# A GNN kernel on one core: GpSimd takes part of the one-hot rows, and the q, k and v products go in f32r parts

## The chip, the cores and the metric

One core of one Trainium2 chip. The metric is the device time of one execution in microseconds; the profiled execution of the kernel before has a span of 487.2 us.

## The reference, cut to what matters

Four graph layers in a row on 512 nodes with 512 features and 16896 edges. What the change touches is the first layer and the table of edges that all layers use:

```
h = relu(layernorm(x))                       # N = 512 nodes, D = 512
q, k, v = h @ Wq + bq, h @ Wk + bk, h @ Wv + bv          # 8 heads of 64
adj = zeros(N, N); adj[src, dst] = 1
scores = q k^T / 8, -1e9 where adj == 0; softmax over heads; times v
... @ Wo, layernorm, feed forward, layernorm
```

Then follow two graph convolutions, one more convolution, and two relational layers that sum 30 basis matrices each into their weights (those matrices are 64 MB, streamed from HBM through the whole kernel).

## The kernel before, in words

**Queues.** Each engine runs one list of instructions written out by hand; they meet in semaphores only. TensorE's list (`pe`) sets the order around the change: `turn` transposes the four blocks of `h`; then comes a loop over 132 chunks of 128 edges (`ECH`). `count(n)` adds one chunk to a table in PSUM bank 7: one bf16 matmul of a 128x128 matrix `hot_d` (a one-hot row of the edge's destination, times a power of two that says which field of the table it belongs to) with a 128x512 matrix `hot_s` (the one-hot row of its source). Both stand in rings of 16 (`HOT`), and a slot is free when the count 16 chunks earlier is done (`hot_used`).

**Who makes the rows.** VectorE (DVE) makes every `hot_s` and, of 132 `hot_d`, the 71 for which `on_act(n)` is false (both in `one_hots`, L722 and L725). ScalarE (ACT) makes the other 61 in two activations each (`distances`, L443, and L468). GpSimd (POOL) makes none; it issues DMAs.

**What stands between the counts.** After the counts 0, 16, 32, ..., 112 TensorE does `qkv_tile(t)`: one 128x512 tile of q (t = 0 to 3) or k (4 to 7) out of four fp32 matmuls (L1280), and then, but for the first, `units(1)`: one MB of basis matrices, read by SyncE's queue into a ring of four (`bring`), in four column-tiled fp32 matmuls (L1197, eight records). ACT takes each finished tile to SBUF (`qk_take`, 14 chunks after it in its own list). After the loop the first half of the table's digits is taken apart by DVE, and the four v tiles are done, two before and two inside the attention steps.

**The start.** DVE computes the norm of `x`, waits for the edge arrays (three DMAs of SyncE's queue, behind the four of `x`), derives the columns from them in eight steps (`edge_step`), then makes `never` (L772) and `bq8` (L774, behind the DMAs of `cols` and `alphas`), and only then the first one-hot rows. ACT copies the transposes to `hT` in fp32 (L395).

**Other products.** All later products of weights already use parts: a float is cut into a high part in f32r and the rest, and hi\*hi + hi\*lo + lo\*hi are three f32r matmuls in place of one in fp32 (`parts_tile`, L1211). ACT makes the high part (L405), DVE the low one (L877).

Of the kernel before, what the change touches and what calls it, by code (L numbers as in the profile page):

```python
# [28 lines left out]
P = 128  # L29
# [20 lines left out]
FIRST_TILE, TILE_EVERY = 0, 16  # L50
TILE_LAG = 14


def act_hots(n):

    return n * 15 // 32
# [44 lines left out]
T_ORDER = ("h1T", "ff1", "ff1_second", "hT2", "agg0", "agg1", "agg2")  # L101
# [12 lines left out]
def build(nc, x, src, dst, etype, weights, rows, cols, alphas, att, basis, scratch, out):  # L114
    with ExitStack() as ctx:
# [71 lines left out]
        x_hi, x_lo = root_hi, root_lo  # L187
        ff1_hi, ff1_lo = (root_hi, root_lo), (y0_hi, y0_lo)
# [83 lines left out]
        with nc.Block() as block:  # L272

            @block.sync
            def _(sp):
# [3 lines left out]
                for i, e in enumerate((src, dst, etype)):  # L279
                    sp.dma_start(edge_i[:, i, :], e).then_inc(sem("edges_loaded"), 16)  # L280
# [35 lines left out]
            def _(pool):  # L316
# [13 lines left out]
                pool.wait_ge(sem("att_loaded"), 16 * 2 * Q)  # L330
                for g in range(1, BATCH):
                    pool.tensor_copy(attw[0:KB, :, g, blk(Q, g)], attw[0:KB, :, 0, 0:Q]).then_inc(
                        sem("att_ready"), 1)
                for i in range(RSLOTS):
                    pool.dma_start(row(ROWS[i]), rows[i, :].partition_broadcast(P)).then_inc(
                        sem(f"row_slot{i}_loaded"), 16)
# [22 lines left out]

                load_weight("f1a")  # L360
                load_weight("f1b")
# [17 lines left out]
            def _(act):  # L379
# [78 lines left out]
                for c in range(C):  # L458
                    turn("hT0", hT, c)
                for n in range(ECH):  # L460
# [10 lines left out]
                    t, at = divmod(n - FIRST_TILE - TILE_LAG, TILE_EVERY)  # L471
                    if at == 0 and 0 <= t < 2 * C:
# [229 lines left out]
            def _(dve):  # L702
# [13 lines left out]
                def one_hots(n):  # L716


                    if n >= HOT:
                        dve.wait_ge(sem("hot_used"), n - HOT + 1)  # L720
                    if not on_act(n):
                        dve.tensor_scalar(hot_d[:, n % HOT, :], iota[:, 0:P], dst_lo[:, n:n + 1],  # L722
                                          weight_f[:, n:n + 1], ALU.is_equal, ALU.mult).then_inc(
                                              sem("hot_ready"), 1)
                    dve.tensor_scalar(hot_s[:, n % HOT, :], iota[:, :], src_f[:, n:n + 1], None,  # L725
                                      ALU.is_equal).then_inc(sem("hot_ready"), 1)
# [19 lines left out]

                for c in range(C):
# [4 lines left out]
                nbias(0, C - 1)  # L752

# [6 lines left out]
                dve.tensor_scalar(rel1, edge_i[:, 2, :], 0.0, None, ALU.not_equal).then_inc(sem("edge_step"), 1)  # L760
                dve.wait_ge(sem("edge_step"), 4)
# [9 lines left out]
                dve.wait_ge(sem("ident"), 2)  # L771
                dve.tensor_scalar(never[:, :], ident[:, :], NEVER, None, ALU.mult).then_inc(sem("never"), 1)  # L772
                dve.wait_ge(sem("cols_loaded"), 32)
                dve.tensor_scalar(bq8[:, :], col("bq", 0, C), HD ** -0.5, None, ALU.mult).then_inc(sem("bq8"), 1)  # L774
# [7 lines left out]
                for n in range(ECH):  # L782
                    one_hots(n)
                    t, at = divmod(n - FIRST_TILE - TILE_LAG, TILE_EVERY)
                    if at == 5 and C <= t < 2 * C:
                        plus_bo(t - C)
# [3 lines left out]
                dve.wait_ge(sem("packed"), 1)  # L790

# [380 lines left out]
            def _(pe):  # L1172
# [93 lines left out]
                def qkv_tile(t):  # L1266

                    which, c = divmod(t, C)
                    w = weight("qkv"[which])
                    if c == 0:  # L1270
                        need_weight(pe, "qkv"[which])
# [5 lines left out]
                    for k in range(C):  # L1277
                        a, b = ((w[:, k, blk(P, c)], hT[:, k, :]) if which < 2 else
                                (hT[:, k, blk(P, c)], w[:, k, :]))
# [3 lines left out]
                first, every = FIRST_TILE, TILE_EVERY  # L1283
# [3 lines left out]
                for n in range(ECH):  # L1287
                    count(n)
                    if n == first:
                        pe.wait_ge(sem("hT0"), C)  # L1290
                    t, at = divmod(n - first, every)
                    if at == 0 and t < 2 * C:
                        qkv_tile(t)
                        if t:
# [338 lines left out]
```

## Time and profile before

| | |
|---|---|
| median of 3 runs | 491.48 us (491.46 to 494.15) |
| profiled execution | 488.97 us, of which 487.2 us span |
| TensorE busy | 442.7 us (91%) |
| VectorE busy | 353.7 us (73%) |
| ScalarE busy | 241.4 us (50%) |
| GpSimd busy | 19.4 us (4%) |
| HBM | 92.45 MB read, 201 GB/s over the span |

The span is what the instructions take from the first to the last; 1.8 us lie around it. The busy shares are means over stages that have different limits, so each stage has to be looked at by itself.

### The profile page before, as it was taken

What the parts mean: (1) busy time and instruction counts of PE and PEld (TensorE: products, weight loads), DVE (VectorE), ACT (ScalarE), POOL (GpSimd) and SP (SyncE); (2) the same over time, 40 slices, a digit from 0 to 9 for tenths busy, and PEclk for the clock granted to TensorE, in tenths of its full rate; (3) what the DMA queues carried; (4) which work ended last, traced back from release to release, by engine and by line L of the source; (5) the groups of instructions that cost most, each with busy time, mean ns of one, the idle gap of its engine ahead of it and who ended that gap; (6) DMA issues with size and microseconds to landing.
All of it is one profiled execution on the core that took longest, in us unless ns stands there. A gap on an engine that the chain in (4) does not pass through costs nothing.

```text
span 487.2 us, 6230 instructions
## 1 busy us (share of the span) xinstructions
PE 442.7 (91%) x2210; PEld 275.4 (57%) x2214; DVE 353.7 (73%) x765; ACT 241.4 (50%) x425; POOL 19.4 (4%) x43
## 2 busy tenths in 40 slices
PE   1699999889877799899999899799989899999997
PEld 1343433344322243577867667578557488888885
DVE  4687887799998869877879684657687767585312
ACT  4697885585786551754225425445562442611210
POOL 3210000001000000100010000000000000000000
PEclk9999999999999999999999999999999899999999
DMA  7992435304999974976149768470797413000002
GB/s 280 339 373 86 173 111 171 109 1 163 367 414 418 394 282 159 398 267 258 77 172 386 275 218 352 174 280 2 291 412 199 172 42 154 3 0 1 0 3 86
DMA packets 18457, 98.16 MB, mean 201 GB/s; under 512 B 3711, under 2 KB 4095, under 8 KB 7935
## 3 DMA queue, kind: packets, MB, share of 16 engines
q1 hardware_dynamic: 14871, 73.58, 40.0%
q0 software_dynamic: 3552, 24.12, 13.3%
q8 instruction: 22, 0.36, 0.3%
q14 instruction: 12, 0.10, 0.1%
HBM read 92.45 MB, written 5.24 MB: 201 GB/s over the span
## 4 chain that ended last, share of the span: by engine, by line
PE 69%; DMA 13%; DVE 11%; ACT 3%; issue 2%; SPq 1%; DVEq 0%; ACTq 0%
PE bank L1211 13%; DMA bring<-in_basis 11%; PE sbank L1528 9%; PE bank L1280 7%; PE sbank L1197 7%; PE bank L1541 6%; PE sbank L1263 6%; PE bank L1423 5%; PE bank L1513 5%; PE bank L1247 3%; DMA alph<-in_alphas 3%; PE bank L1197 3%; PE sbank L1387 2%; PE sbank L1181 2%; PE sbank L1247 2%
## 5 line engine op out<-in xcount | busy, mean ns | idle before, releaser
L725 DVE TENSOR_SCALAR cnt<-iota_row,edge_f 128x512 bf16<-128x512 f16 x132 | 41.5, 352 | 4.5 <-PE sbank L1263 4.5
L1197 PE MATMUL sbank<-bring,attw 120*32 120x512 f32 x320 | 40.4, 616 | 2.2 <-DMA bring<-in_basis 2.2
L1197 PE MATMUL bank<-bring,attw 120*32 120x512 f32 x192 | 24.3, 618 | 8.2 <-DMA bring<-in_basis 8.0
L383 ACT ACTIVATE stat<-stat 128x1 f32<-128x1 f32 x32 | 6.5, 202 | 51.0 <-DVE stat L733 51.0
L1263 PE MATMUL sbank<-cnt,adjT 128*128 128x512 bf16 x128 | 29.4, 381 | 1.9 <-DVE cnt L725 1.3
L1280 PE MATMUL bank<-hT,wring 128*128 128x512 f32 x64 | 30.5, 622 | 0.0
L468 ACT ACTIVATE adjT<-distance,edge_w,edge_f 128x128 bf16<-128x128 bf16 x61 | 29.3, 480 | 1.4 <-PE sbank L1263 1.4
L1130 DVE SCALAR_TENSOR_TENSOR y_lo<-sbank,gate,y_hi 128x512 fp32r<-128x512 f32 x16 | 11.8, 750 | 22.5 <-ACT y_hi L652 22.5
L443 ACT ACTIVATE distance<-iota_row,edge_f 128x128 bf16<-128x128 f16 x61 | 24.4, 401 | 5.1 <-DVE edge_f L769 3.4
L722 DVE TENSOR_SCALAR adjT<-iota_row,edge_f,edge_w 128x128 bf16<-128x128 f16 x71 | 22.2, 313 | 6.3 <-remote 6.3
L1211 PE MATMUL bank<-hT_hi,w_hi 128*128 128x512 f32 x64 | 25.5, 398 | 1.0 <-DVE y_hi L958 0.8
L411 ACT ACTIVATE s<-bank,colsb 128x512 f32<-128x512 f32 x24 | 16.4, 684 | 18.8 <-PE bank L1211 18.8
L1181 PE MATMUL sbank<-ident,hr 128*128 128x128 f32 x64 | 11.9, 321 | 14.9 <-ACT hr L453 7.5
L1211 PE MATMUL bank<-hT_hi,w_lo 128*128 128x512 f32 x64 | 25.0, 391 | 0.0
L1211 PE MATMUL bank<-hT_lo,w_hi 128*128 128x512 f32 x64 | 24.9, 390 | 0.0
L1528 PE MATMUL sbank<-w_hi,xT_hi 128*128 128x512 f32 x64 | 24.9, 389 | 0.0
L1528 PE MATMUL sbank<-w_hi,xT_lo 128*128 128x512 f32 x64 | 24.9, 389 | 0.0
L1528 PE MATMUL sbank<-w_lo,xT_hi 128*128 128x512 f32 x64 | 24.9, 389 | 0.0
L1263 PEld LDWEIGHTS sbank<-cnt,adjT 128*128 128x128 bf16 x132 | 12.3, 98 | 21.7 <-DVE cnt L725 4.4
L1311 PE MATMUL sbank<-qkw 64*128 64x256 f32 x128 | 18.1, 402 | 5.8 <-DVE s L899 5.0
L490 ACT ACTIVATE s<-s 128x1024 f32<-128x1024 f32 x16 | 16.8, 1058 | 11.9 <-DVE s L899 11.4
L652 ACT ACTIVATE y_hi<-sbank,gate 128x512 fp32r<-128x512 f32 x16 | 10.8, 688 | 23.8 <-PE sbank L1528 23.8
(224 smaller groups left out, 1046.3 us busy)
## 6 DMA issues: line engine op xcount, KB each, us to landing
bring<-in_basis SPq DMA_DIRECT2D x63, 1024.0 KB, 8.1
wring<-in_weights POOLq DMA_DIRECT2D x8, 1024.0 KB, 8.8
w_scratch<-stage SPq DMA_DIRECT2D x64, 64.0 KB, 6.9
hT<-in_weights POOLq DMA_DIRECT2D x4, 1024.0 KB, 5.3
landing<-in_weights POOLq DMA_DIRECT2D x4, 1024.0 KB, 8.5
qkw<-w_scratch POOLq DMA_DIRECT2D x2, 2048.0 KB, 8.1
rring<-in_rows POOLq DMA_DIRECT2D x12, 256.0 KB, 8.0
xr<-in_x SPq DMA_DIRECT2D x4, 256.0 KB, 4.0
```

Source lines behind the costliest of these rows:

```text
L443: act.activation(distance[:, i % 2, :], iota[:, 0:P], ACT.Abs, scale=-1.0, bias=dst_lo[:, n:n + 1]).then_inc(sem("distance"), 1)
L468: act.activation(hot_d[:, n % HOT, :], distance[:, i % 2, :], ACT.Relu, scale=minus_w[:, n:n + 1], bias=weight_f[:, n:n + 1]).then_inc(sem ...
L725: dve.tensor_scalar(hot_s[:, n % HOT, :], iota[:, :], src_f[:, n:n + 1], None, ALU.is_equal).then_inc(sem("hot_ready"), 1)
L1197: mm = pe.matmul(unit_bank(b)[32 * j:32 * j + 32, :], attw[0:KB, u // UNITS, g, :], bring[0:KB, u % BATCH, j, :], start=(g == 0), stop=(g ...
L1211: mm = pe.matmul(bank[c][:, :], lhs[:, k, blk(P, c)], rhs[:, k, :], start=(k == 0 and i == j), stop=(k == C - 1 and i == 1))
L1247: mm = pe.matmul(bank[first_bank + c][:, :], x[:, k, blk(P, c)].bitcast(dt), counts[:, k, :], start=(k == 0 and i == 0), stop=(k == C - 1 ...
L1263: pe.matmul(bank[7][:, :], hot_d[:, n % HOT, :], hot_s[:, n % HOT, :], start=(n == 0), stop=(n == ECH - 1)).then_inc(sem("hot_used"), 1)
L1280: mm = pe.matmul(bank[at][:, :], a, b, start=(k == 0), stop=(k == C - 1))
L1423: mm = pe.matmul(bank[c][:, :], (ff1_hi, ff1_lo)[i][k // C][:, k % C, blk(P, c)], weight_parts("f2a" if k < C else "f2b")[j][:, k % C, :], ...
L1513: mm = pe.matmul(bank[c][:, :], (xT_hi, xT_lo)[i][:, k, blk(P, c)], (root_hi, root_lo)[j][:, k, :], start=(k == 0 and i == j), stop=False)
L1528: mm = pe.matmul(bank[C + c][:, :], (xT_hi, xT_lo)[i][:, k, blk(P, c)], (w_hi, w_lo)[j][:, rel * C + k, :], start=(k == 0 and i == j), sto ...
L1541: mm = pe.matmul(bank[c][:, :], counts[:, k, blk(P, c)], y[:, k, :].bitcast(dt), start=False, stop=(rel == RELS - 1 and k == C - 1 and i = ...
```

## The change

1. Of the 132 `hot_d`, ACT makes `n * 5 // 16` = 41 and GpSimd the other 91; DVE makes none. TensorE waits for `pool_hot_ready` too.
2. `qkv_tile` is twelve f32r matmuls in place of four fp32 ones. The low parts of `h` are made by DVE (`h0T_lo`), the high ones by ACT, which now turns block c right after the norm of block c + 1. The weight of q is cut by GpSimd (high) and DVE (low) ahead of the loop, those of k and v by ACT and DVE inside the loop.
3. The tiles of q and k come after the counts 0, 8, 16, 28, 46, 64, 84 and 104; ACT takes each 7 chunks later in its list.
4. The three edge DMAs are issued by ACT's queue, ahead of its first square root. The five row DMAs of GpSimd and the copies of `attw` stand inside its loop. `never` and `bq8` move to chunk 8 of DVE's loop.
5. The loads of `f1a` and `f1b` change places; DVE waits for all k tiles before it writes the digits.

```diff
-FIRST_TILE, TILE_EVERY = 0, 16
-TILE_LAG = 14
+TILE_AT = (0, 8, 16, 28, 46, 64, 84, 104)
+TILE_LAG = 7
 def act_hots(n):
-    return n * 15 // 32
+    return n * 5 // 16
...
+        h0_hi, h0_lo = y1_lo, hT_r
+        qkv_parts = {"q": (y0_hi, w0_hi), "k": (y0_lo, w0_lo), "v": (w0_hi, w1_hi)}
...
@@ SyncE's list @@
-                for i, e in enumerate((src, dst, etype)):
-                    sp.dma_start(edge_i[:, i, :], e).then_inc(sem("edges_loaded"), 16)
...
@@ GpSimd's list @@
+                need_weight(pool, "q")
+                for k in range(C):
+                    pool.tensor_copy(qkv_parts["q"][0][:, k, :], weight("q")[:, k, :]).then_inc(sem("q_hi"), 1)
+                pool.wait_ge(sem("edge_step"), 8)
+                for n in range(ECH):
+                    if n == HOT:
+                        pool.wait_ge(sem("att_loaded"), 16 * 2 * Q)
+                        for g in range(1, BATCH):
                            pool.tensor_copy(attw[0:KB, :, g, blk(Q, g)], ...)
+                    i, at = divmod(n - 2 * HOT, 4)
+                    if at == 0 and 0 <= i < RSLOTS:
+                        pool.dma_start(row(ROWS[i]), ...)
+                    if on_act(n):
+                        continue
+                    if n >= HOT:
+                        pool.wait_ge(sem("hot_used"), n - HOT + 1)
+                    pool.tensor_scalar(hot_d[:, n % HOT, :], iota[:, 0:P], dst_lo[:, n:n + 1],
+                                       weight_f[:, n:n + 1], ALU.is_equal, ALU.mult).then_inc(
+                                           sem("pool_hot_ready"), 1)
...
@@ ACT's list @@
+                def high_part(name, k):
+                    if k == 0:
+                        need_weight(act, name)
+                    if name == "v":
+                        act.wait_ge(sem("q_psum"), C)
+                    act.copy(qkv_parts[name][0][:, k, :], weight(name)[:, k, :]).then_inc(sem("kv_hi"), 1)
+                for i, e in enumerate((src, dst, etype)):
+                    act.dma_start(edge_i[:, i, :], e).then_inc(sem("edges_loaded"), 16)
+                    if c:
+                        turn("hT0", h0_hi, c - 1)
+                turn("hT0", h0_hi, C - 1)
+                    if n - 2 * HOT in (0, 2, 4, 6):
+                        high_part("k", (n - 2 * HOT) // 2)
+                    if n - 4 * HOT - 12 in (0, 4, 8, 12):
+                        high_part("v", (n - 4 * HOT - 12) // 4)
...
@@ DVE's list @@
-                    if not on_act(n):
-                        dve.tensor_scalar(hot_d[:, n % HOT, :], ...)
+                def low_part(name, k):
+                    hi, lo = qkv_parts[name]
+                    dve.wait_ge(*((sem("q_hi"), k + 1) if name == "q" else
+                                  (sem("kv_hi"), "kv".index(name) * C + k + 1)))
+                    dve.tensor_tensor(lo[:, k, :], weight(name)[:, k, :], hi[:, k, :].bitcast(F32),
+                                      ALU.subtract).then_inc(sem("qkv_parts"), 1)
+                def h0T_lo(c):
+                    dve.wait_ge(sem("T_hi"), c + 1)
+                    dve.tensor_tensor(h0_lo[:, :, blk(P, c)], bank[4 + c % 2] ..., h0_hi ..., ALU.subtract)
@@ h0T_lo(0) stands after nbias, h0T_lo(1) after edge step 4; before the loop: @@
+                low_part("q", 0); low_part("q", 1); h0T_lo(2); h0T_lo(3); low_part("q", 2); low_part("q", 3)
+                    if n == HOT // 2:  # never, bq8
+                    if n - 2 * HOT - 8 in (0, 2, 4, 6):
+                        low_part("k", (n - 2 * HOT - 8) // 2)
+                    if n - 5 * HOT in (0, 4, 8, 12):
+                        low_part("v", (n - 5 * HOT) // 4)
+                    if n - 112 in (0, 4, 8, 12):
+                        plus_bo((n - 112) // 4)
+                dve.wait_ge(sem("k_psum"), C)   # ahead of the digits
...
@@ TensorE's list @@
-                    pe.wait_ge(sem("hot_ready"), 2 * (n + 1) - act_hots(n + 1))
+                    pe.wait_ge(sem("hot_ready"), n + 1)
+                    pe.wait_ge(sem("pool_hot_ready"), n + 1 - act_hots(n + 1))
                     for k in range(C):
-                        mm = pe.matmul(bank[at][:, :], a, b, start=(k == 0), stop=(k == C - 1))
+                        pe.wait_ge(sem("qkv_parts"), which * C + k + 1)
+                        for i, j in ((0, 0), (0, 1), (1, 0)):
+                            ...
+                            mm = pe.matmul(bank[at][:, :], lhs, rhs, start=(k == 0 and i == j),
+                                           stop=(k == C - 1 and i == 1))
```

## Rows read from the trace of the kernel before

**Rows 1.** Busy time by stretch: us, then each engine's busy time (instructions), clock, DMA

```profile
17.90:84.30 66.40, 65.25 (x252) 26.48 (x260) 53.70 (x208) 52.80 (x130) 4.04 (x8) 1.00 0.56 198
...
121.00:175.00 54.00, 44.56 (x327) 16.58 (x324) 47.56 (x53) 38.48 (x47) 0.00 (x0) 0.97 0.99 400
```

**Rows 2.** Chain of waits, 17.6 to 28 us: start, us, what

```profile
4.49 13.20 DMA alph<-in_alphas
...
17.71 0.17 DVE bq L774
...
18.41 0.61 PE sbank L1263
19.02 5.15 PE bank L1280 x8
```

**Rows 3.** Chain of waits over the whole span, some of its longest pieces

```profile
27.62 3.43 PE bank L1280 x8
31.06 1.00 PE sbank L1197 x8
32.21 3.40 PE sbank L1263 x15
...
278.16 11.15 PE bank L1211 x48
```

**Rows 4.** Groups by line, 18.4 to 84.2 us: busy us, mean ns, idle before and its releaser

```profile
L725 DVE TENSOR_SCALAR cnt<-iota_row,edge_f 128x512 bf16<-128x512 f16 x131 | 41.1, 352 | 4.5 <-PE sbank L1263 4.5
...
L468 ACT ACTIVATE adjT<-distance,edge_w,edge_f 128x128 bf16<-128x128 bf16 x61 | 29.3, 480 | 1.4 <-PE sbank L1263 1.4
L443 ACT ACTIVATE distance<-iota_row,edge_f 128x128 bf16<-128x128 f16 x59 | 23.6, 400 | 1.7
L722 DVE TENSOR_SCALAR adjT<-iota_row,edge_f,edge_w 128x128 bf16<-128x128 f16 x70 | 21.9, 313 | 6.3 <-remote 6.3
```

**Rows 5.** Timeline of VectorE, 20 to 24 us, while its loop runs freely

```profile
20.51 0.32 DVE L722 TENSOR_SCALAR adjT<-iota_row,edge_f,edge_w 128x128 bf16<-128x128 f16 x1
20.73 0.62 DVE L725 TENSOR_SCALAR cnt<-iota_row,edge_f 128x512 bf16<-128x512 f16 x2
21.25 0.32 DVE L722 TENSOR_SCALAR adjT<-iota_row,edge_f,edge_w 128x128 bf16<-128x128 f16 x1
```

**Rows 6.** Timeline of GpSimd, 0 to 30 us

```profile
1.59 0.51 POOL L320 MEMSET zeros<- 128x512 bf16 x1
...
2.44 0.29 POOL L324 TENSOR_SCALAR_AFFINE_SELECT ident<-ident 128x128 f32<-128x128 f32 x1 [0.16 <-POOL ident L322]
...
21.80 1.11 POOL L332 COPY attw<-attw 120x16 f32<-120x16 f32 x3 [16.59 <-DMA attw<-in_att]
22.86 2.98 POOL L335 DMA_DIRECT2D rring<-in_rows x5
```

**Rows 7.** Timeline, 278 to 285 us: a weight is cut into its parts

```profile
278.62 2.21 ACT L405 CAST w_hi<-hT 128x512 fp32r<-128x512 f32 x4
...
279.73 2.49 DVE L877 TENSOR_TENSOR w_lo<-hT,w_hi 128x512 fp32r<-128x512 f32 x4
```

**Rows 8.** Timeline of the start, 0 to 22 us

```profile
9.35 0.21 DVE L738 TENSOR_SCALAR stat<-stat 128x1 f32<-128x1 f32 x1 [0.16 <-ACT stat L383]
12.50 0.23 DVE L755 CAST edge_f<-edge_i 128x132 f32<-128x132 int32 x1 [2.94 <-DMA edge_i<-in_etype]
...
13.91 0.23 DVE L769 TENSOR_SCALAR edge_f<-edge_w 128x132 f32<-128x132 f32 x1
```

**Rows 9.** DMA issues at 2.9 to 3.4 us: KB, us to landing

```profile
wring<-in_weights POOLq DMA_DIRECT2D x1, 1024.0 KB, 7.8
```

**Rows 10.** Chain of waits, 84 to 125 us

```profile
87.12 3.63 PE bank L1280 x8
...
93.02 1.23 DVE softmax_tmp L824
...
124.88 10.20 DMA bring<-in_basis
```

More of the change, by code:

```diff
@@ L329, in _ @@
                     pool.dma_start(weight(WEIGHTS[i]), weights[i]).then_inc(sem(f"weight_{i}_loaded"), 16)
[L330 to L336, printed above, removed]
+                need_weight(pool, "q")
[6 more added lines that the diff above has]
+                        for g in range(1, BATCH):
+                            pool.tensor_copy(attw[0:KB, :, g, blk(Q, g)], attw[0:KB, :, 0, 0:Q]).then_inc(
+                                sem("att_ready"), 1)
+                    i, at = divmod(n - 2 * HOT, 4)
+                    if at == 0 and 0 <= i < RSLOTS:
+                        pool.dma_start(row(ROWS[i]), rows[i, :].partition_broadcast(P)).then_inc(
+                            sem(f"row_slot{i}_loaded"), 16)
+                    if on_act(n):
[5 more added lines that the diff above has]
+                                           sem("pool_hot_ready"), 1)
                 def load_weight(name):
@@ L358, in load_w @@
                     pool.dma_start(qkw[:, :, :], scratch[layer]).then_inc(sem("w_loaded"), 16)
+                load_weight("f1b")
                 load_weight("f1a")
-                load_weight("f1b")
                 load_row("g2", "v")
@@ L457, in _ @@
                 distances(0)
-                for c in range(C):
-                    turn("hT0", hT, c)
                 for n in range(ECH):
@@ L752, in _ @@
                 nbias(0, C - 1)
+                h0T_lo(0)
                 dve.wait_ge(sem("edges_loaded"), 48)
@@ L770, in _ @@
                 dve.wait_ge(sem("iota"), 1)
[L771 to L774, printed above, removed]
+                low_part("q", 0)
+                low_part("q", 1)
+                h0T_lo(2)
+                h0T_lo(3)
+                low_part("q", 2)
+                low_part("q", 3)
                 def plus_bo(c):
@@ L783, in _ @@
                     one_hots(n)
-                    t, at = divmod(n - FIRST_TILE - TILE_LAG, TILE_EVERY)
-                    if at == 5 and C <= t < 2 * C:
-                        plus_bo(t - C)
+                    if n == HOT // 2:
+                        dve.wait_ge(sem("ident"), 2)
+                        dve.tensor_scalar(never[:, :], ident[:, :], NEVER, None, ALU.mult).then_inc(sem("never"), 1)
+                        dve.wait_ge(sem("cols_loaded"), 32)
+                        dve.tensor_scalar(bq8[:, :], col("bq", 0, C), HD ** -0.5, None, ALU.mult).then_inc(
+                            sem("bq8"), 1)
+                    if n - 2 * HOT - 8 in (0, 2, 4, 6):
[4 more added lines that the diff above has]
+                        plus_bo((n - 112) // 4)
                 dve.wait_ge(sem("hot_used"), ECH)
@@ L1268, in qkv_tile @@
                     which, c = divmod(t, C)
-                    w = weight("qkv"[which])
-                    if c == 0:
-                        need_weight(pe, "qkv"[which])
+                    w = qkv_parts["qkv"[which]]
                     if which == 1:
@@ L1277, in qkv_tile @@
                     for k in range(C):
-                        a, b = ((w[:, k, blk(P, c)], hT[:, k, :]) if which < 2 else
-                                (hT[:, k, blk(P, c)], w[:, k, :]))
-                        mm = pe.matmul(bank[at][:, :], a, b, start=(k == 0), stop=(k == C - 1))
+                        pe.wait_ge(sem("qkv_parts"), which * C + k + 1)
+                        for i, j in ((0, 0), (0, 1), (1, 0)):
+                            h = (h0_hi, h0_lo)[i]
+                            lhs, rhs = ((w[j][:, k, blk(P, c)], h[:, k, :]) if which < 2 else
+                                        (h[:, k, blk(P, c)], w[j][:, k, :]))
+                            mm = pe.matmul(bank[at][:, :], lhs, rhs, start=(k == 0 and i == j),
+                                           stop=(k == C - 1 and i == 1))
                     mm.then_inc(sem("qkv"[which] + "_psum"), 1)
-                first, every = FIRST_TILE, TILE_EVERY
                 pe.wait_ge(sem("ident"), 2)
@@ L1288, in _ @@
                     count(n)
-                    if n == first:
+                    if n == 0:
                         pe.wait_ge(sem("hT0"), C)
[L1291 to L1294, printed above, removed]
+                    if n in TILE_AT:
+                        qkv_tile(TILE_AT.index(n))
+                        if n:
                             units(1)
```

13 lines of the change are left out of this document (7 added, 6 removed).

## The prediction

> **What bounds the kernel now.** I read four views in this order. First the busy time by stretch [rows 1]: from 17.9 to 84.3 us TensorE is busy 65.25 of 66.4 us, VectorE 53.7, ScalarE 52.8, GpSimd 4.0. This is the stretch of the loop over chunks, and TensorE sets its length. Then the chain of waits [rows 2, 3]: from 18.41 us on it runs on TensorE alone, in a pattern of a q or k tile (3.43 us), a unit of basis matrices (1.00) and some 16 counts (15 take 3.40, about 0.22 each). The sum closes: 132 counts at 0.22 = 29; seven tiles at 3.43 and a first one of 5.15 = 29.2; eight units = 8; together 66 us. Then the groups by line [rows 4]: VectorE's one-hot rows wait for free ring slots (4.5 and 6.3 us idle), so the makers of rows are ahead. Last, the start [rows 2, 8]: the loop could not begin before 18.41 us, because `bq8` (17.71) waited for a tiny DMA that landed 13.20 us after its issue. Behind the loop follow the attention steps, and from 124.88 us on a stretch in which the DMAs of the basis are the limit [rows 1, 10]: 0.99 of the DMA engines, begun by TensorE's fourth group of units. It begins when the attention step before it is done and lasts as long as its bytes do, so an earlier end of the loop moves all that follows by the same amount.
>
> **Tiles in f32r parts (on the path).** 48 f32r matmuls took 11.15 us [rows 3], 0.232 each, so 12 take 2.79 us where four fp32 ones took 3.43: 0.64 less a tile. The first tile ran slow before (5.15 us [rows 2], 1.72 more than its kin), right after TensorE's idle time of the start; that idle time stays, so I keep the surcharge. Eight tiles: 8 x 0.64 = **-5.1 us**.
>
> **The v tiles.** Four more. The first (3.63 us at 87.12 [rows 10]) is on the chain, which reaches the first maximum at 93.02: **-0.8 us**. The other three stand beside VectorE's chain of softmax steps: nothing.
>
> **Making the parts (beside, while the cover holds).** ACT copies eight blocks for k and v at 0.55 [rows 7], 2.21 for four, 4.4 us, and loses 20 of its 61 rows, which are worth 0.40 + 0.48 = 0.88 busy each [rows 4], about -17 us. VectorE makes low parts at 0.62 each [rows 7]: eight inside the loop, 5.0 us, and loses 71 rows at 0.22 [rows 5], 15.8 us. If there is no contention both become freer, and cost nothing.
>
> **The start.** VectorE is done with the norm at 9.56 [rows 8]. From there it has: four low parts of the transposes (4 x 0.62 = 2.5), the eight steps on edges (12.50 to 14.14, 1.6), four low parts of q (2.5), one row of sources (0.27). Without a gap the first count starts at 16.4. Do the inputs come in time? The weight of q landed at 2.96 + 7.8 = 10.8 [rows 9]; GpSimd's copy of 128x512 costs at least the 0.51 of a memset of that size [rows 6] and I allow twice that, so its fourth block stands at 13 to 15 us, and is used last, at about 15.5. The edge arrays, landed by 12.5 before, are now issued about 1.9 us earlier, and wanted at 10.2. The last transposes wait in turn for VectorE's first two low parts, which costs a gap of some tenths. GpSimd starts its rows here too and may delay the low parts (below). So the first count comes between 16.4 and 18.4; I take 17.4, **-1.0 us**. `never` and `bq8` are moved behind row 8, where the late DMA is covered by 8 counts and a tile.
>
> **The rows of GpSimd (the open price).** 91 `tensor_scalar` of 128x128. The trace has none on this engine. Nearest from below: the same shape in one pass, affine_select, 0.29 us, with VectorE idle; from above: three COPYs of 16 columns beside a running VectorE took 1.11 us, 0.37 each [rows 6], and 112 further columns at the rate of the memset (0.51 for 512) add 0.11: 0.48. Two column operands and a change of type could double the 0.48, so the ends are 0.29 and 1.0. I take 0.45. What can the loop bear? The tight part is from count 28 on: before it tiles stand close (0, 8, 16, 28), and the ring of 16 fills. From there TensorE has 104 counts (22.5), five tiles (13.9) and five units (5.0), 41.3 us, in which the makers must bring chunks 44 to 131, 88 of them. GpSimd has 60 or 61 of these, so it may take 41.3 / 60 = 0.69, less the row DMAs that fall in (five at 0.6 [rows 6], in part before): **0.67 us each**. 0.45 fits. At the start it makes 11 rows, then waits for the DMAs of `attw`, there by 21.8 [rows 6]; count 16 comes after two more tiles, at about 29 us, so that wait is covered. ACT: 41 rows spaced by 0.81 to 0.88, 36 us, plus 4.4 of parts, 5.5 of `qk_take`, 0.6 of staging: 47 of 60 us.
>
> **Waits on TensorE.** Each count gets one more wait. 61 of the counts had a second one already and the 16 counts of a group still took about 0.22 each [rows 3], so I take nothing; the upper bound is 132 pieces of 0.05 like the handoffs in the chain, 6.6 us, were none of them hidden. The exchange of `f1a` and `f1b` and the wait for the k tiles ahead of the digits cost nothing: `f1a` is first cut three attention steps after both loads were issued, and the last k tile now ends 27 counts before the digits.
>
> **Sum.** -5.1 - 0.8 - 1.0 = -6.9 us. The profiled execution took 488.97 (487.2 span and 1.8 around); 482.1 after it. The median of the runs lies 2.5 above the profiled one, so 491.48 - 6.9 = **484.6 us**.
>
> **Rival 1: VectorE and GpSimd take turns.** Three copies of 16 columns took 0.37 each beside VectorE, where 128 columns took 0.29 in its absence, so each waited 0.1 to 0.25 us, about one instruction of VectorE [rows 5, 6]; VectorE's own spacing (0.74 for three instructions) did not grow visibly, but those copies were tiny. If a GpSimd row holds VectorE back for its whole length x, the tight part needs 88 x 0.26 + 5.0 + 2.5 of other VectorE work (a little less of it falls in: 6.0) + 60x = 28.9 + 60x against 41.3: free up to x = 0.21, +5.0 us at 0.29, +9.8 at 0.37. That gives 489.6 to 494.4. Against it: part of both instructions' length is not traffic (a one-column memset already takes 0.1 in this trace), so the exclusive shares are perhaps 0.2 and 0.15 to 0.2, and the sum stays just inside 41.3. The Trainium skill, page "SBUF — State Buffer", section "Who interferes with whom", speaks for this rival: it says that VectorE in its two-port modes, and a VectorE instruction with two SBUF inputs against a GpSimd one that reads SBUF, lock GpSimd out for the whole instruction and the other way round. By that rule taken literally the result is 489.6 or above; the copies above agree with the one direction, and no row shows the other.
>
> The Trainium skill, page "GPSIMD Engine Reference", section "Engine selection", calls one-input work on GpSimd roughly line-rate; by it the price would lie at the low end, and GpSimd itself would not be the bound.
>
> **Rival 2: GpSimd is simply slow (the other side).** If a row costs p alone, the tight part lasts 60p + 1.2 for the row DMAs. Break-even with the gain of 6.9 is at p = 0.78, slower by over 1% begins at 0.87; at 1.0 the loop ends 19.9 us later than forecast, 504.5. For it: a copy of only 16 columns took 0.41 in the mean on this engine. Against it: the affine_select of full shape in 0.29.
>
> **Rival 3: the start or the waits eat it.** The low parts of q come late behind GpSimd's copies and rows (first count at 19 to 20), or the third wait slows the counts by some hundredths: +2 to +6, 486.6 to 490.6.
>
> **How the numbers follow.** Chances: forecast 0.50 (482.8 to 486.5), rival 1 0.26 (486.5 to 494), rival 2 0.16 (491 to 505), rival 3 0.08. About 1% (4.9 us) is what a measurement of this kernel can tell from none. Faster by over 1% is below 486.6: the forecast's 0.50 and 0.03 of rival 1. Within 1%: 0.29. Slower, above 496.4: 0.18, most of rival 2 and the worst of rival 1. The range of 8 in 10 leaves out the fast tail and the slower half of rival 2: 482.5 to 497.
>
> **What would show it.** A tile's twelve matmuls in 2.8 us; the loop from about 17.4 to 78 us with TensorE busy over 95% of it. GpSimd's spacing of rows: below 0.67 and idle on `hot_used` for the forecast; near 0.69 or more with TensorE waiting on GpSimd's rows for rival 2. For rival 1, VectorE's spacing of rows of sources above 0.40 in the stretch without TensorE's pauses, and TensorE idle before counts. The first maximum at about 86.1 us, which was 93.02; all stages from 121 us on unchanged in length but shifted. If those later stages change their length, or the weight of q lands later than 10.8, the prediction is wrong in a way that I have not priced.

## The result and the profile after

The changed kernel took 507.71 us in the median of four runs (506.25 to 509.92), the kernel before 492.58 us (491.46 to 494.15) beside it: ratio 1.031, 95% interval 1.0254 to 1.0363. It is slower by 3.1%, where 484.6 us had been forecast and 497 was the upper end. The profiled execution took 508.46 us, its span is 506.7, 19.5 more than before.

Busy time by stretch of the kernel after (length, PE, PEld, DVE, ACT, POOL, then clock, DMA share, GB/s), which answers to [rows 1]:

```profile
18.00:40.00 22.00, 21.72 (x92) 13.48 (x93) 14.85 (x47) 9.74 (x23) 21.90 (x29) 1.00 0.73 287
40.00:60.00 20.00, 16.18 (x69) 7.32 (x68) 13.87 (x36) 10.73 (x26) 19.84 (x24) 0.91 0.48 158
60.00:80.00 20.00, 15.70 (x72) 7.21 (x71) 14.93 (x42) 11.94 (x30) 20.00 (x24) 1.00 0.34 110
80.00:100.00 20.00, 15.70 (x53) 6.80 (x53) 8.75 (x25) 6.45 (x16) 20.00 (x23) 0.83 0.18 62
```

GpSimd is busy in 81.7 of these 82 us. TensorE is busy nearly all the time up to 40 us and in some four fifths of it from there on; its granted clock falls to 0.91 and 0.83 in two of the stretches in which it is kept waiting, where it was 1.00 in [rows 1]. VectorE and ScalarE do less than before. So the loop has a new bound, and the chain of waits of the kernel after (start, us, what) says from when:

```profile
18.28 0.61 PE sbank L1316
18.89 5.12 PE bank L1334 x12
24.01 1.81 PE sbank L1316 x8
25.82 2.73 PE bank L1334 x12
...
35.12 2.70 PE sbank L1316 x12
37.81 2.77 PE bank L1334 x12
40.58 1.00 PE sbank L1249 x8
41.58 1.42 PE sbank L1316 x6
43.00 3.35 POOL adjT L348 x3
46.35 0.56 POOL rring L342
...
46.97 1.71 POOL adjT L348 x2
48.68 0.55 POOL rring L342
...
49.28 51.08 POOL adjT L348 x58
...
100.49 0.59 PE sbank L1316 x2
...
104.01 2.95 PE bank L1334 x12
...
109.24 1.23 DVE softmax_tmp L876
```

Up to 43.00 us the pattern is that of [rows 3], on TensorE alone. At count 35 the stock of rows is used up, and from there the chain runs on GpSimd: 63 rows and two row DMAs up to 100.35 us. The groups by line of the page give the price of a row (busy us, mean ns, idle before and its releaser):

```profile
L348 POOL TENSOR_SCALAR adjT<-iota_row,edge_f,edge_w 128x128 bf16<-128x128 f16 x91 | 82.3, 912 | 1.2 <-DVE edge_f L808 0.9
L749 DVE TENSOR_SCALAR cnt<-iota_row,edge_f 128x512 bf16<-128x512 f16 x132 | 45.4, 407 | 20.8 <-PE sbank L1316 20.7
L1316 PE MATMUL sbank<-cnt,adjT 128*128 128x512 bf16 x132 | 36.8, 392 | 16.9 <-DVE cnt L749 10.2
```

912 ns, and GpSimd never waits for a free slot: its idle time before rows is the 1.2 us at the start. VectorE waits 20.7 us for slots instead, so its rows are ahead. The third group names VectorE as the releaser of TensorE's waits, though VectorE was well ahead (48 of its rows stood at 43 us, where count 35 was due); a count waits for several makers, and the chain shows the one that was late. The 91 rows began at 14.36 us: with 82.3 us of rows, five row DMAs at 0.55 and the copies of `attw` the engine is done at 100.4.

The last count starts at 100.7 us (before 83.8), the first maximum at 109.24 (93.02 [rows 10]). Of the 19.5 us of span, 16.2 are there already; the rest comes further on, told with the last three runs below.

### The profile page after: what moved, and what is told of

Read it like the earlier page. It is cut to its first block, busy times and chain, and to the rows that moved or that the text cites. A ratio compares the mean times of both kernels' runs of the same rounds, so it can differ in the third digit from the quotient of the medians.

```text
span 506.7 us, 6399 instructions
## 1 busy us (share of the span) xinstructions
PE 450.5 (89%) x2262; PEld 289.9 (57%) x2262; DVE 358.1 (71%) x710; ACT 229.3 (45%) x393; POOL 103.6 (20%) x138
## 4 chain that ended last, share of the span: by engine, by line
PE 58%; DVE 17%; POOL 11%; DMA 7%; ACT 4%; issue 2%; DVEq 0%; SPq 0%; ACTq 0%
PE bank L1263 11%; POOL adjT L348 11%; PE sbank L1581 9%; DMA bring<-in_basis 6%; PE bank L1594 6%; PE sbank L1249 5%; PE bank L1476 4%; PE bank L1566 4%; PE bank L1299 3%; PE bank L1334 3%; PE bank L1249 2%; PE sbank L1440 2%; DVE stat L754 2%; PE sbank L1316 2%; PE sbank L1233 2%
## 5 line engine op out<-in xcount | busy, mean ns | idle before, releaser
L348 POOL TENSOR_SCALAR adjT<-iota_row,edge_f,edge_w 128x128 bf16<-128x128 f16 x91 | 82.3, 912 | 1.2 <-DVE edge_f L808 0.9
L749 DVE TENSOR_SCALAR cnt<-iota_row,edge_f 128x512 bf16<-128x512 f16 x132 | 45.4, 407 | 20.8 <-PE sbank L1316 20.7
L1316 PE MATMUL sbank<-cnt,adjT 128*128 128x512 bf16 x132 | 36.8, 392 | 16.9 <-DVE cnt L749 10.2
L1364 PE MATMUL sbank<-qkw 64*128 64x256 f32 x128 | 22.0, 470 | 6.4 <-DVE s L951 5.6
L1364 PEld LDWEIGHTS sbank<-qkw 64*128 64x128 f32 x128 | 13.3, 223 | 18.5 <-issue 11.0
L518 ACT ACTIVATE s<-s 128x1024 f32<-128x1024 f32 x16 | 16.9, 1058 | 13.1 <-DVE s L951 12.5
L680 ACT ACTIVATE y_hi<-sbank,gate 128x512 fp32r<-128x512 f32 x16 | 10.8, 688 | 23.8 <-PE sbank L1581 23.8
L1249 PEld LDWEIGHTS sbank<-bring,attw 120*32 120x32 f32 x320 | 8.2, 111 | 21.9 <-issue 18.3
L356 POOL DMA_DIRECT2D hT<-in_weights x4 | 2.1, 533 | 87.3 <-DVE w_lo L929 87.3
```

Source lines behind the costliest of these rows:

```text
L348: pool.tensor_scalar(hot_d[:, n % HOT, :], iota[:, 0:P], dst_lo[:, n:n + 1], weight_f[:, n:n + 1], ALU.is_equal, ALU.mult).then_inc(sem("p ...
L518: act.activation(sc, sc, ACT.Exp).then_inc(sem("exped"), 1)
L1249: mm = pe.matmul(unit_bank(b)[32 * j:32 * j + 32, :], attw[0:KB, u // UNITS, g, :], bring[0:KB, u % BATCH, j, :], start=(g == 0), stop=(g ...
L1316: pe.matmul(bank[7][:, :], hot_d[:, n % HOT, :], hot_s[:, n % HOT, :], start=(n == 0), stop=(n == ECH - 1)).then_inc(sem("hot_used"), 1)
L1364: pe.matmul(sbank[:, place_of(h), :], kT[at:at + HD, h // 2, blk(P, m)], qT[at:at + HD, h // 2, blk(NH, half_n)], start=(a == 0), stop=Fal ...
```

## The experiments

Small kernels first, for the price of a row; then parts of the change; then other shares of the work.

**m1, the price by itself.** This kernel leaves out the network and only copies `x`; besides, GpSimd makes rows of several kinds, alone and beside VectorE. A column operand is one value for each partition, read from a tile; an immediate is a constant in the instruction.

```diff
+ # A 24x tensor_scalar 128x128 f16->bf16, two columns   B one column   C immediate
+ # D 24x tensor_copy   E 8x as A, 128x512   F as A, fp32
+ # G as A beside VectorE's rows of 512   H as A beside VectorE's fp32 tensor_tensor
```

> Not the network: a small kernel that only copies x to the output and times GpSimd's row by itself, 24 rows of 128 columns in each stretch. A: as in the changed kernel (f16 in, bf16 out, two column operands), VectorE idle. B: one column operand. C: one immediate. D: a copy. E: 512 columns. F: fp32 in and out. G: as A, beside VectorE making 128x512 rows of sources. H: as A, beside fp32 subtractions of VectorE. Theory 1 (the row is dear in itself): A is spaced by 0.8 to 0.9 us, G by no more than 0.15 more, and B, C or D show which part of the instruction costs it. Theory 2 (GpSimd and VectorE take turns): A is spaced by 0.3 to 0.6 us and only G and H come to 0.9; VectorE's rows in G are spaced by far more than the 0.26 us they have alone.

The timeline of that kernel (start, us, engine, operation, count), GpSimd's blocks in order and VectorE's beside them:

```profile
2.21 18.58 POOL L70 TENSOR_SCALAR pa<-iota_row,dst,w 128x128 bf16<-128x128 f16 x24
20.88 13.87 POOL L76 TENSOR_SCALAR pb<-iota_row,dst 128x128 bf16<-128x128 f16 x24
34.84 13.78 POOL L81 TENSOR_SCALAR pc<-iota_row 128x128 bf16<-128x128 f16 x24
48.69 5.76 POOL L86 CAST pd<-iota_row 128x128 bf16<-128x128 f16 x24
54.56 16.45 POOL L91 TENSOR_SCALAR pe<-iota_row,dst,w 128x512 bf16<-128x512 f16 x8
71.11 18.58 POOL L97 TENSOR_SCALAR y<-iota,dst,w 128x128 f32<-128x128 f32 x24
...
89.73 4.29 DVE L117 TENSOR_SCALAR va<-iota_row,dst 128x512 bf16<-128x512 f16 x16 [89.73 <-POOL y L97]
94.05 19.39 DVE L121 TENSOR_SCALAR vb<-iota_row,dst 128x512 bf16<-128x512 f16 x64
94.12 21.53 POOL L103 TENSOR_SCALAR pg<-iota_row,dst,w 128x128 bf16<-128x128 f16 x24 [4.43 <-DVE va L117]
...
118.21 12.68 DVE L130 TENSOR_TENSOR vc<-xr,iota 128x512 f32<-128x512 f32 x20
```

Alone a row costs 18.58 / 24 = 0.774 us with two column operands, 0.58 with one or with an immediate, and a copy of the same shape 0.24. Four times the columns cost 2.06 us: (2.056 - 0.774) / 384 = 3.34 ns a column. From f16 to bf16 or in fp32 it costs the same. Beside VectorE's rows it is 21.53 / 24 = 0.90, as in the kernel, and VectorE's go from 4.29 / 16 = 0.268 to 19.39 / 64 = 0.303: three of them to a GpSimd row, each held back by 0.035, so a GpSimd row delays VectorE by 0.1. Of the 0.912 us in the kernel 0.774 are the instruction's own, and 0.13 to 0.14 come from company. Beside fp32 subtractions seven rows took 13.20 us, 1.9 each, and VectorE kept its 0.634.

**e1, only the rows.** The kernel before with GpSimd's 91 rows and ACT's 41, its fp32 tiles left as they were.

```diff
-    return n * 15 // 32
+    return n * 5 // 16
 # GpSimd's loop as in the change; DVE's hot_d removed
+                    pe.wait_ge(sem("hot_ready"), n + 1)
+                    pe.wait_ge(sem("pool_hot_ready"), n + 1 - act_hots(n + 1))
```

> The kernel before, fp32 tiles and its own order of tiles, with only the makers changed: GpSimd 91 rows of destinations, ScalarE 41, VectorE none. If GpSimd's pace alone sets the loop (91 rows at 0.88 to 0.91, from about 14 us on, plus 3 us of DMA issues), the loop ends at 98 to 102 us instead of 84 and the time is 505 to 510 us, the same as the whole change. If the turns with the added fp32 subtractions were a good part of the cost, it would be well below, 498 or less.

505.88 us against 490.67, ratio 1.030 (1.0225 to 1.0374). The rows alone bring as long a time as the whole change. But the last count is at 95.3 us, 5.4 earlier than with the whole change and earlier than I had expected; the first maximum is at 104.56, and some 4 of the 15 us come behind it. The group of rows:

```profile
L345 POOL TENSOR_SCALAR adjT<-iota_row,edge_f,edge_w 128x128 bf16<-128x128 f16 x90 | 76.7, 860 | 0.3
```

GpSimd doesn't wait for slots here either (0.3 us of idle time), and a row costs 860 ns in place of 912; 52 ns in each of 91 rows are 4.7 of the 5.4 us. What e1 leaves out is the work on the parts, fp32 subtractions of VectorE among it. In m1 three of those went by in one GpSimd row of 1.9 us; twelve on the parts of weights would so make four rows dearer by 1 us each, an estimate of 4 us. No run takes this work away alone.

**e2, only the parts; e3, three makers.** The kernel after, but with the rows shared otherwise.

```diff
+def pool_hots(n):
+    return (n - act_hots(n)) * 4 // 7        # e2: 0
-    return n * 5 // 16
+    return n * 11 // 32                      # e3; e2 keeps 5 // 16
+ # DVE makes what is neither ACT's nor GpSimd's
```

> The changed kernel, but VectorE makes the 91 rows of destinations of GpSimd (ScalarE keeps 41); all the rest of the change stands. If the f32r parts and the new start are worth what I took for them (6.9 us) and only GpSimd's rows undid it: 485 to 488 us, with the loop's end at 78 to 80 us; VectorE's own work in the tight part (88 x 0.26 + 60 x 0.22 + 6 = 42 us against TensorE's 41) costs about 1. If the parts bring nothing (waits on TensorE, the start), 491 or more.

> The changed kernel with the rows of destinations dealt three ways: ScalarE 45, GpSimd 49, VectorE 38. GpSimd's 49 rows at 0.9 us are 44 us in a loop of 60, so it no longer sets the pace; VectorE has 132 x 0.3 + 38 x 0.24 + 8 = 57 us of 60. Theory 1 (own price, little lock): TensorE is the bound again, 484 to 487 us. Theory 2 (turns, each GpSimd row holds VectorE back for much of its length): VectorE falls behind, 490 us or more.

e2: 493.62 us, ratio 1.0054 (1.0015 to 1.0092). I had expected a gain, and it is a small loss. Its groups by line from 15 to 100 us:

```profile
L765 DVE TENSOR_SCALAR cnt<-iota_row,edge_f 128x512 bf16<-128x512 f16 x132 | 43.4, 353 | 0.4 <-remote 0.4
L762 DVE TENSOR_SCALAR adjT<-iota_row,edge_f,edge_w 128x128 bf16<-128x128 f16 x91 | 28.7, 315 | 2.3 <-PE sbank L1333 2.3
```

VectorE makes 223 rows here and is idle before them for 2.7 us in all; before it was 10.8 [rows 4]. Its rows stand on the chain of waits from 17.7 to 28.5 us. So VectorE is what TensorE waits for, as GpSimd was, and the tiles' gain has nowhere to go: last count at 84.4 us. e3 with 45 rows by ACT, 49 by GpSimd and 38 by VectorE: 489.22 us, ratio 0.998 (0.995 to 1.0009), last count at 82.2 us, between my two theories. A GpSimd row took 1152 ns there:

```profile
L360 POOL TENSOR_SCALAR adjT<-iota_row,edge_f,edge_w 128x128 bf16<-128x128 f16 x49 | 56.0, 1152 | 8.4 <-PE sbank L1333 5.8 <-remote 1.6 <-DVE edge_f L824 0.8
```

**e7, a cheaper row.** The kernel after with one comparison in GpSimd's row; it leaves out the multiplication by the weight, so the table holds no usable counts, and the kernel's own test of the table is changed to let it go on.

```diff
-                                       weight_f[:, n:n + 1], ALU.is_equal, ALU.mult).then_inc(
+                                       None, ALU.is_equal).then_inc(
...
-                dve.tensor_scalar(flag[:, :], bank[0][0:1, 0:1], float(EDGES), None, ALU.is_equal).then_inc(
+                dve.tensor_scalar(flag[:, :], bank[0][0:1, 0:1], 0.0, None, ALU.is_ge).then_inc(
```

> The changed kernel as it is (GpSimd 91 rows), but its row is one comparison with one column operand: the multiplication by the edge's weight is left out, and the test of the table is made to pass, so the counts are meaningless and only the time counts. In the small kernel this row took 0.58 us alone in place of 0.77. If GpSimd's own price is all of the loss, the loop ends at 91 x 0.65 + 3 + 14.4 = 77 to 84 us and the time falls by some 15 us to that of the kernel before or below. If something else in the change costs (third wait on TensorE, f32r tiles, the start), more than 498 us remain.

494.87 us (three runs), ratio 1.007 (1.0034 to 1.0106). The group of rows from 15 to 100 us:

```profile
L348 POOL TENSOR_SCALAR adjT<-iota_row,edge_f 128x128 bf16<-128x128 f16 x91 | 65.3, 731 | 2.3 <-PE sbank L1316 2.1
```

912 - 731 = 181 ns less for each of 91 rows is 16.5 us, and the last count starts 15.3 us earlier (100.7 to 85.4). By this the price moves the end of the loop as 85 rows would (15.3 / 0.181), near to all 91 and not the 60 of the part that I had called tight. GpSimd now waits 2.1 us for free slots, which it never did before.

**m2, what VectorE does to other kinds.** Again a small kernel that only copies `x`; all of GpSimd's blocks run beside VectorE's rows.

```diff
+ # beside VectorE: 16x one column, 16x immediate, 24x copy, 5x 128x512, 12x two columns
```

> The second small kernel, each stretch of GpSimd beside a free run of VectorE's 128x512 rows (spaced 0.30 us there). In the first one a row with two column operands lasted exactly three VectorE instructions (0.906 beside rows of 0.302, 1.90 beside subtractions of 0.634). Theory (each operand that GpSimd fetches waits for one VectorE instruction to end): one column operand 0.60 us, an immediate 0.30 to 0.60, a copy 0.30, 512 columns 2.1 to 2.4, and beside VectorE rows of 128 columns (0.22 us) a row with two operands 0.77 to 0.88. Rival (a constant surcharge of 0.13 us for company): 0.71, 0.70, 0.37, 2.2 and 0.90.

The rows with one column took 10.64 / 16 = 0.66 us, with an immediate 0.63, with 512 columns 11.53 / 5 = 2.3 and with two columns, beside VectorE's rows of 128 columns, 0.89: 0.05 to 0.25 more than alone and not rounded up to whole instructions of VectorE, so the theory that GpSimd falls in step with VectorE fell, and the rival of a constant 0.13 did too. The copies did something else. Timelines of GpSimd and VectorE, from 32 us:

```profile
32.15 6.38 POOL L81 CAST pd<-iota_row 128x128 bf16<-128x128 f16 x1 [2.31 <-DVE va L110]
```

```profile
32.00 6.38 DVE L113 TENSOR_SCALAR ve<-iota_row,dst 128x512 bf16<-128x512 f16 x24
```

One copy that costs 0.24 alone lasted through all 24 rows that VectorE had queued; the other 23 ran after them.

**e4 and e6, ACT takes more.** As e3, with other shares (ACT, GpSimd, VectorE): 49, 20, 63 and 49, 0, 83.

```diff
-    return n * 11 // 32
+    return n * 12 // 32
-    return (n - act_hots(n)) * 4 // 7
+    return (n - act_hots(n)) * 1 // 4        # e6: 0
```

> The changed kernel with ScalarE making 49 rows of destinations, GpSimd 20 and VectorE 63. In the small kernel a GpSimd row advanced in step with VectorE (three VectorE instructions long) and delayed it by 0.10 us. Theory (every maker below the pace of TensorE): VectorE has 132 x 0.26 + 63 x 0.22 + 8 + 20 x 0.1 = 58 us, ScalarE 49 x 0.81 + 10.5 = 50, GpSimd 20 x 1.1 = 22, TensorE 60: the loop ends at 78 to 80 us and the time is 4 to 6 us below the kernel before. Rival (the ring of 16 is too short for VectorE at 97% of TensorE's pace, so its pauses are not made up): 82 us and 1 to 3 us below.

> As the variant with few rows on GpSimd, but GpSimd makes none: ScalarE 49, VectorE 83. VectorE has 132 x 0.26 + 83 x 0.22 + 8 = 60.6 us against TensorE's 60 and no slack. If VectorE's total sets the time, it ends the loop at 81 to 83 us, and is 1 to 3 us slower than with 20 rows on GpSimd; if GpSimd's rows cost VectorE as much as they save it (0.22 each), the two are equal.

e6: 491.40 us, ratio 1.0013 (0.9976 to 1.005), last count at 83.4 us, so with no rows on GpSimd the change gives nothing that can be told. e4: last count at 82.8 us, and yet 495.40 us, ratio 1.0082 (1.0053 to 1.0111). I had expected a gain of 4 to 6 us, and e6 to be the slower of the two. The profiled execution of e4 was the fastest of its five runs (491.59 us), so no trace of mine shows where the others lost their time.

**e5 and e10, the high parts moved.** Shares 53, 19, 60; the high parts of q are made by ACT in the start, those of k and v by GpSimd in its loop. In VectorE's list the third low part of q stands before the last one of `h`. e10 is e5 word for word, on another chip.

```diff
-                    pool.tensor_copy(qkv_parts["q"][0][:, k, :], weight("q")[:, k, :])
+                    act.copy(qkv_parts["q"][0][:, k, :], weight("q")[:, k, :])
+                    if n - 2 * HOT in (-8, -6, -4, -2):      # GpSimd
+                        high_part("k", (n - 2 * HOT + 8) // 2)
```

> The changed kernel with ScalarE 53 rows, GpSimd 19, VectorE 60; GpSimd makes the high parts of k and v (0.6 us a block) in place of ScalarE, ScalarE those of q in place of GpSimd, so that nothing of GpSimd runs beside VectorE's steps on the edges. Theory (GpSimd's copies stretched those steps from 0.22 to 0.6 us and cost the start what I expected of it): the first count comes at 17.0 to 17.6 us in place of 18.3, and the time is 1 us below the variant with few rows on GpSimd. Rival: the transposes' low parts bound the start and nothing moves.

> The variant with the high parts moved once more, word for word, in five rounds: its first ratio was 0.996 (0.9914 to 1.0006), while its loop ended 3.8 us earlier and its first maximum came 4.5 us earlier than in the profile of the kernel before. If that gain holds to the end, the ratio is 0.991 to 0.995; if the later stages give it back, 0.998 or more.

Ratios 0.996 (0.9914 to 1.0006) and 0.9969 (0.9936 to 1.0002). That lies between my two theories for e10. The start is the clear part. Timeline of VectorE's steps on the edge arrays, the kernel after with GpSimd's casts of the weight of q beside them:

```profile
11.04 2.40 POOL L332 CAST y_hi<-wring 128x512 fp32r<-128x512 f32 x4 [5.80 <-DMA wring<-in_weights]
11.06 0.22 DVE L794 TENSOR_SCALAR dst_part<-edge_i 128x132 int32<-128x132 int32 x1
11.20 0.63 DVE L796 TENSOR_SCALAR dst_part<-edge_i 128x132 int32<-128x132 int32 x1
11.76 0.64 DVE L798 TENSOR_SCALAR edge_f<-edge_i 128x132 f32<-128x132 int32 x1
```

and e10 without them:

```profile
10.63 0.22 DVE L818 TENSOR_SCALAR dst_part<-edge_i 128x132 int32<-128x132 int32 x1
10.77 0.22 DVE L820 TENSOR_SCALAR dst_part<-edge_i 128x132 int32<-128x132 int32 x1
10.91 0.22 DVE L822 TENSOR_SCALAR edge_f<-edge_i 128x132 f32<-128x132 int32 x1
```

Here it is VectorE that is held up: a step beside the casts lasts about as long as a cast (2.40 / 4 = 0.60 us). With the casts gone the first count starts at 16.8 us in e10 and 17.2 in e5, where it was 18.0 to 18.3 in three profiles with GpSimd's casts and 91 rows (e7, b3 and the kernel after); the last one at 80.5 and 80.0, the first maximum at 89.1 and 88.5.

**e8, more for GpSimd; e9, the tiles spread.** Both from e5: GpSimd also adds the row of `bo` to `h` in four fp32 sums; or ACT 57, GpSimd 18, VectorE 57 and tiles spaced more widely.

```diff
+ # e8
+                        pool.tensor_tensor(hr[:, c, :], hr[:, c, :], row("bo"), ALU.add)
+ # e9
-TILE_AT = (0, 8, 16, 28, 46, 64, 84, 104)
+TILE_AT = (0, 8, 16, 28, 47, 67, 88, 110)
```

> The variant with the high parts moved, and GpSimd also adds the row of bo to h at chunks 68, 76, 84 and 92 in place of VectorE at 112 to 124. Theory (VectorE at 97% of TensorE's pace, its last sums stand where TensorE has only counts left): the last count 1 to 2 us earlier, at 78 to 79 us, 485 to 488 us in the median, 3 us or more below the kernel before. Rival (GpSimd's fp32 sums hold VectorE back as long as they save it): no change from the variant without, 489.

> The variant with the high parts moved, with four more rows on ScalarE (57; GpSimd 18, VectorE 57) and the last four tiles spread evenly to the loop's end (after counts 47, 67, 88 and 110 in place of 46, 64, 84 and 104), so that TensorE leaves fewer bare counts at the end, which VectorE can't follow. Theory (VectorE's rate is enough in the mean, and only the tail starves TensorE): the last count at 78.5 to 79.5 us in place of 80.0, 487 to 489 us, 2.5 to 4 us below the kernel before. Rival (the mean rate is the limit): the last count stays at 80 us or later.

e8: ratio 0.9988 (0.9959 to 1.0016), last count at 82.7 us, where I had expected 78 to 79 and e10 has 80.5: the sums took work from VectorE, but its rows of sources became slower, 383 ns in the mean after 366 in e5. e9: ratio 0.9974 (0.9938 to 1.0011), last count at 80.0 us, as in e5. The spacing and the four more rows of ScalarE together don't move the end. That is what the rival said (the makers' mean rate is the limit), but with two things changed at once e9 doesn't prove it.

**b1, b2, b3, the same kernels again.** All versions above that end their loop earlier gained less than that. Between the fourth group of units and the next in the chain of waits the kernel before has 69.2 us, the one after 71.1 and e10 70.4. Is that the spread from one execution to the next?

```diff
 # b1, b2: the kernel before; b3: the kernel after; nothing changed
```

> The kernel before, word for word, for a second profile. In its first profile the stretch from the first units after the loop to the 28th unit took 59.1 us from the 12th on, and in ten profiles of variants 59.9 to 62.3, although nothing in that stretch differs but its start. Theory (the stretch varies from execution to execution, and the first profile of before, 488.97 us against a median of 491, had a short one): 60 to 62 us here. Rival (an earlier or later end of the loop changes how the stretch goes, and a part of each gain is given back there): 59.1 again, within 0.5.

> The kernel before, word for word, a third profile. As for the second: 60 to 62 us from the 12th to the 28th unit if the stretch varies by itself, 59.1 within 0.5 if it does not.

> The changed kernel, word for word, a second profile. The rows of GpSimd: 91 at 0.90 to 0.92 us, the last count at 100 to 101.5 us again (the loop does not vary, all of the spread of the time stands behind it); 506 to 510 us.

The two ends of the stretch in the chain of waits, b1 and then b3:

```profile
122.57 3.62 PE bank L1197 x32
191.00 3.62 PE bank L1197 x32
```

```profile
136.78 3.62 PE bank L1249 x32
206.77 3.62 PE bank L1249 x32
```

68.4 us (b2 68.5) and 70.0. Three profiles of the kernel before lie at 68.4 to 69.2, and the twelve of the kernel after and its variants at 69.9 to 72.3. Two profiles of one kernel differ by up to 1.1 there (71.1 and 70.0 for the kernel after), but the two groups don't overlap, so it is not spread alone: some 1 to 3 us are given back there. Which change does it is not shown. All twelve kernels have another loop, and all of them, e1 too, issue the five row DMAs and the copies of `attw` inside GpSimd's loop; no run has only the one or the other. The stretch after it is spread: from the units at 289 us to the `x32` row at 357 the kernel before took 67.7, 69.2 and 69.0 us, the one after 69.4 and 69.3. b3 reproduces the loss, 506.47 us against 490.98 and 489.97, with 909 ns a row and the last count at 100.0 us.

## Why the prediction was wrong, step by step

**What bounds the kernel.** Right: the chain was on TensorE in the loop, and with other shares it ends earlier (e10: last count at 80.5 against 83.8), though by less than the 5 to 6 us forecast.

**Tiles in parts.** Right. On the chain each took 2.73 to 2.77 us, forecast 2.79. The first took 5.12 against 5.15 [rows 2] in this profile, which looks as if nothing had been gained there, but it varies from one execution to the next. The same tile in b3:

```profile
18.70 4.23 PE bank L1334 x12
```

The chains of ten profiles with twelve f32r matmuls have 3.9 to 5.1 us there, 4.5 in the mean; four with fp32 (the kernel before, b1, b2, e1) have 4.8 to 5.7, 5.3 in the mean. So by the means the first tile gained its 0.64 too, and that nothing of it shows in one profile was chance. What varies is how many of the twelve matmuls start 0.43 us apart, and not 0.23. Two tiles of the loop show the same 0.43 at their start, at 48.9 to 51.3 and 85.1 to 88.8 us, after counts for which TensorE had waited; there the granted clock is 0.50, the lower of its two levels (1.2 and 2.4 GHz). In the first tile the clock row reads 1.00, so for that tile the cause is not shown. The v tile is right within 0.1: 2.95 after 3.63 [rows 10].

**Making the parts.** Right that ACT has room (it went to 53 and 57 rows in e10 and e9). The cover for VectorE was GpSimd: with all 91 rows on VectorE it is gone, and e2 has no gain.

**The start.** Forecast 17.4, measured 18.28, against 18.41 before. The norm was done at 10.41 instead of 9.56, the first block of `x` having landed at 4.45 us instead of 3.96 and VectorE having waited for the second (the edge DMAs are issued beside them now; no run moves these alone). Then GpSimd's casts stretched three of VectorE's steps as shown, by 1.2 us in sum. I had allowed for a delay by rows, not by casts; with 16.8 and 17.2 in e10 and e5 the 17.4 was sound without them.

**Waits on TensorE.** Right: eight counts took 1.81 us, 0.226 each as in [rows 3], each with the added wait.

**The rows of GpSimd: the step that failed.** I took 0.45 us and measured 0.91. The value was taken from copies and an affine_select as the nearest rows, and neither was near: m1 shows that on this engine the operands set the price (copy 0.24, one column 0.58, two 0.77). The upper end, 1.0, held, and rival 2 named the mechanism. How much a dear row costs was mis-sized too. Rival 2's formula, 60p + 1.2, gives 55.2 us at p = 0.9 against 41.3, 13.9 more than forecast: 489 + 7 = 496 for the profiled execution, and 508.5 came. It assumed a full ring at count 28, that is, 30 rows of GpSimd by 36 us; from 14.4 us on GpSimd had made 22 by then. So the engine never gets ahead of its ring, and all 91 rows count: with 14.4 us of start and 3.7 of other work, 18.1 + 91p = 100 at 0.9, against a forecast end of 78. The point up to which it is free, (78 - 18.1) / 91 = 0.66, agrees with my 0.67; the slope above it is 91, not 60. e7 measured 85.

**Rival 1.** The contention is real, but it acts the other way round. What it takes from VectorE, 0.1 us for a row, is small. What it takes from GpSimd, 0.13 to 0.14 us for a row, falls on the engine at the bound: with m1's 0.774 the same sum gives 18.1 + 91 x 0.774 = 88.5 us for the end of the loop, with 0.912 it gives 101. By this estimate 12.6 us of the delay are company; alone, a row's own price would have ended the loop some 5 us later than before (83.8). So a price measured alone would have told the direction, and under a third of the 16.9 us. The Trainium skill, page "SBUF — State Buffer", section "Who interferes with whom", tells of a lock for the whole instruction. For GpSimd's casts beside VectorE's steps (0.22 to 0.64 us) the traces agree; the copy (6.38 us) was shut out too, but through 24 instructions and not one. For rows with column operands no such lock shows: VectorE's went from 0.268 to 0.303 beside GpSimd ones of 0.9. Whether these rows run in one of the two-port modes that the section speaks of, no run here shows. The other page I had named, "GPSIMD Engine Reference", section "Engine selection", calls one-input work roughly line-rate; the copy agrees (0.24 us, VectorE's row of that shape 0.22 [rows 5]), the one-input row with two column operands doesn't, 0.774.

**Later stages only shifted.** Nearly: of 19.5 us, 16.2 are there at the first maximum, 1.9 come in the DMA-bound stretch (69.2 to 71.1) and 1.7 between 289 and 357 us, which b1 and b2 show as spread. The prediction had named a change of length there as a sign of something not priced. What makes the former longer in every variant stays open. In the traces single units and single attention steps jump by 2 to 3 us, as if the loads and the steps of some 10 us paced each other anew; no run here isolates that.

**A better version.** e5 and e10, the same kernel on two chips, came to 0.9960 and 0.9969 of the kernel before. Each interval just reaches 1: a gain of 0.3 to 0.4%, not clear of none, of the 1.4% that I had forecast.

## What to carry to other kernels

A price taken from another kind of instruction on the same engine is no estimate: measure the very instruction, with its operands, alone and beside its neighbours, before an engine gets 91 of them. When work moves to an idle engine, lay out its whole list from its first instruction to its last against the deadline; if it is late from the start, a tight part worked out with full buffers understates the loss. Contention of a seventh of a row is worth a line of its own in the sum, if it falls on the engine that then bounds. And a saving on the engine at the bound is only worth what the next engine can follow: here VectorE had only 10.8 us of idle time before its rows, and e2 used it up.

## What the runs showed of the hardware

- GpSimd's `tensor_scalar` of 128x128: 0.774 us with two column operands, 0.58 with one or an immediate, 0.24 for a cast copy, alike for f16 to bf16 and for fp32 (two column operands); 3.34 ns for each further column (m1).
- Company costs each kind differently: beside VectorE's bf16 rows 0.90 us, beside its fp32 `tensor_tensor` 1.9 us, and a cast copy was held off for 6.38 us by 24 rows in a row, while GpSimd's fp32 casts stretched VectorE's 0.22 us steps to 0.64.
- A GpSimd row cost 860 ns in e1, 912 in the kernel after, 1152 in e3 and 1249 to 1325 in e4, e5, e8, e9 and e10, where VectorE makes rows of 128 and of 512 columns in turn. A busy VectorE alone doesn't explain it: beside an unbroken run of one kind of its rows m1 and m2 had 0.90 and 0.89. No run isolates the rest.
- f32r matmuls of 128x512 started 0.23 us apart in the loop, and 0.43 apart in part or all of the first tile and where the granted clock was 0.50; the first tile took 3.9 to 5.1 us in ten profiles.
